# Reordering the projection and mix stages: variances in two halves among the casts, later projection, mixes two images ahead

## What is computed

```python
# projection stage: normalize over the 128 channels of each pixel, add, and project to 16 channels
xn = (x - mean(x)) / sqrt(var(x) + eps)      # per pixel, over channels
s = x + xn                                   # kept for the mix stage
pm = einsum('bchw,mc->bmhw', xn, w_in)       # 128 -> 16 channels
# (a stage between the two turns pm into xe: FFT, gain, inverse FFT)
# mix stage: back to 128 channels, add, normalize again
x1 = s + einsum('bmhw,cm->bchw', xe, w_out)  # 16 -> 128 channels
tn = (x1 - mean(x1)) / sqrt(var(x1) + eps)   # input of the next stage
total = tn.sum(pixels)                       # for the routing of the experts
```

## Time and profile before

| | us |
|---|---|
| median of 3 runs (lowest, highest) | 3659.25 (3657.81, 3667.75) |
| the profiled execution, its own time | 3660.29 |
| its span in the trace | 3658.5 |
| projection stage, about | 0 to 210 |
| mix stage, about | 412 to 641 |

### The profile page before, as it was taken

The page is one execution under the profiler, slowest core; times in us unless marked ns, Lnnn a source line. Parts: engine busy times, 40 slices in busy tenths (PEclk is TensorE's granted clock), DMA queues, the critical chain, the costliest instruction groups (busy, mean ns, idle before and its releaser), DMA issues. The chain is left out here.

```text
span 3658.5 us, 67013 instructions
## 1 busy us (share of the span) xinstructions
PE 3166.6 (87%) x27077; PEld 1711.9 (47%) x27136; DVE 1684.6 (46%) x2348; ACT 1527.2 (42%) x2263; POOL 810.3 (22%) x694
## 2 busy tenths in 40 slices
PE   5655676399999985999997879999999999999999
PEld 1155422255555542566665434546463545545444
DVE  5724256567677541111112254545454645545453
ACT  3411244167776661111223334545453444445433
POOL 2410232134444421111110112121212111121221
PEclk7767666699999985999998889999999999999999
DMA  5421364313334323777777311313132231313000
GB/s 187 154 75 23 121 257 196 157 46 138 147 147 164 153 115 123 187 212 214 214 207 236 123 56 52 127 46 128 51 104 81 76 109 41 110 43 125 12 12 23
DMA packets 192538, 438.59 MB, mean 120 GB/s; under 512 B 33341, under 2 KB 100157, under 8 KB 183741
## 3 DMA queue, kind: packets, MB, share of 16 engines
q1 hardware_dynamic: 192356, 436.20, 35.9%
HBM read 247.40 MB, written 188.75 MB: 119 GB/s over the span
## 5 line engine op out<-in xcount | busy, mean ns | idle before, releaser
L2113 DVE TENSOR_TENSOR d_hid_scaled<-d_hid_scaled,d_ps 128x512 f32<-128x512 f32 x512 | 331.3, 684 | 605.7 <-PE d_ps L1800 553.6
L1789 PE MATMUL d_ps<-d_hid_scaled,d_w 128*128 128x512 f32 x1024 | 526.4, 596 | 8.0 <-DVE d_X L2119 3.8
L1974 ACT ACTIVATE d_hid_scaled<-d_ps,d_b 128x512 f32<-128x512 f32 x512 | 349.9, 686 | 382.0 <-PE d_ps L1778 375.6
L1517 PE MATMUL c_ps<-c_pad,c_weight 32*32 32x512 f32 x13824 | 475.2, 601 | 26.2 <-ACT c_pad L1469 18.9
L1517 PEld LDWEIGHTS c_ps<-c_pad,c_weight 32*32 32x32 f32 x13824 | 287.1, 103 | 214.1 <-issue 129.7
L1776 PE MATMUL d_ps<-d_tnh,d_w1h 128*128 128x512 f32 x512 | 296.5, 579 | 9.2 <-ACT d_hid_scaled L1974 9.2
L1148 PE MATMUL b_ps<-b_hid,b_w2s 128*128 128x512 f32 x512 | 261.6, 595 | 0.0
L2061 POOL CAST d_tnh<-d_TN 128x512 fp32r<-128x512 f32 x64 | 39.9, 623 | 972.7 <-PE d_ps L1778 935.4
L1578 DVE COPY c_pad<-c_P 128x1024 f32<-128x1024 f32 x48 | 33.4, 696 | 414.9 <-PE c_ps L1517 379.2
L1789 PEld LDWEIGHTS d_ps<-d_hid_scaled,d_w 128*128 128x128 f32 x1024 | 195.5, 191 | 44.5 <-DVE d_hid_scaled L2113 2.3
L1469 ACT ACTIVATE c_pad<-c_P 128x1024 f32<-128x1024 f32 x48 | 51.8, 1080 | 392.7 <-PE c_ps L1517 372.0
(11 more groups left out here) (270 smaller groups left out, 5858.7 us busy)
## 6 DMA issues: line engine op xcount, KB each, us to landing
scratch_qkv<-b_qkv SPq DMA_DIRECT2D x64, 768.0 KB, 3.5
c_P<-scratch_qkv SPq DMA_DIRECT2D x192, 256.0 KB, 4.7
scratch_agg<-c_out SPq DMA_DIRECT2D x192, 256.0 KB, 5.0
d_buf<-scratch_qkv SPq DMA_DIRECT2D x96, 512.0 KB, 4.4
d_buf<-scratch_agg SPq DMA_DIRECT2D x96, 512.0 KB, 3.8
p_X<-in_x SPq DMA_DIRECT2D x8, 2048.0 KB, 7.5
scratch_s<-p_X SPq DMA_DIRECT2D x8, 2048.0 KB, 6.3
m_X<-scratch_s SPq DMA_DIRECT2D x8, 2048.0 KB, 7.7
```

The lines of the kernel that those rows point to most:

```text
L1517: end = nc.tensor.matmul(ps[on(i), k * QUADS + h, :].rearrange("p (b r w) -> p b r w", b=2, w=HB), weight[k][on(q), 2 * r + x, on(h)], pad ...
L1789: nc.tensor.matmul(moe_bank, w2[:, e, :], scaled[n % 3][:, :], start=False, stop=(e == E - 1)).then_inc(moe_pe, 1)
L1974: nc.scalar.activation(hid[n % 3][:, :], hid_bank(n), ACT.Gelu, bias=b1[:, n % E:n % E + 1]).then_inc(hid_done, 1)
L2113: nc.vector.tensor_tensor(scaled[n % 3][:, :], hid[n % 3][:, :], spread_bank(n), ALU.mult).then_inc(scaled_done, 1)
```

## The change

No instruction of the computation is added or removed. In the projection stage:

- `squares` gets 8 buffers instead of 4
- TensorE's body becomes: 8 casts of the mean of b, variances 0 to 3, inverse casts 0 to 3 of b-1, variances 4 to 7, inverse casts 4 to 7 of b-1, means of b+1, projection of image b-2 (before: b-1)
- ScalarE does deviations ahead of split 0 of b+1, and reads image b-2
- VectorE inverts after five scalings instead of six

In the mix stage:

- `X` and `XE` hold four images instead of three, and image b+4 is loaded when image b is stored and centred
- image b+2 is mixed in the body of image b, in pairs: after casts 0 to 3, after casts 4 to 7, after inverse casts 4 to 7, and at the end. Images 0 and 1 are mixed before the first body
- variances in two halves, with the inverse casts 0 to 3 of b-1, means of b+1, and inverse casts 4 to 7 between them
- ScalarE does split 1 of b-1 at the head of the body, and its reads in pairs among the squares
- VectorE scales all of image b-1 and does join 0 of b+1 before it inverts
- SyncE stores `X` of image b+2 and then `TN` of image b-1 in the turn of image b

The diff, cut to its core:

```diff
@@ projection: TensorE
                     for c in range(NCH):
                         norm.cast_mean(pe, b, c, mean_free(b))
+                    norm.variances(pe, b, range(4))
+                    for c in range(4):
+                        norm.cast_inverse(pe, b - 1, c, inverse_free(b - 1))
+                    norm.variances(pe, b, range(4, NCH))
+                    for c in range(4, NCH):
+                        norm.cast_inverse(pe, b - 1, c, inverse_free(b - 1))
                     if more:
                         means(b + 1)
-                    for c in range(4):
-                        norm.cast_inverse(pe, b - 1, c, inverse_free(b - 1))
-                    norm.variances(pe, b)
-                    for c in range(4, NCH):
-                        norm.cast_inverse(pe, b - 1, c, inverse_free(b - 1))
-                    project(b - 1)
+                    if b >= 2:
+                        project(b - 2)
@@ projection: ScalarE
+                    norm.deviations(act, b, eps)
                     if more:
                         norm.split(act, b + 1, 0)
-                    norm.deviations(act, b, eps)
                     norm.split(act, b, 1)
+                    if b >= 2:
+                        read(b - 2)
@@ projection: VectorE
-                    scale(b - 1, range(6))
+                    scale(b - 1, range(5))
                     norm.invert(dve, b)
-                    scale(b - 1, range(6, NCH))
+                    scale(b - 1, range(5, NCH))
@@ mix: SyncE
                 def next_load(b):
                     sp.wait_ge(x1_stored, b * 16 + 16)
                     norm.wait_centred(sp, b, NCH - 1)
-                    sp.wait_ge(loaded, b * 80 + 240)
-                    passed(sp)
-                    load(b + 3)
+                    sp.wait_ge(loaded, b * 80 + 320)
+                    load(b + 4)
...
+                sp.wait_ge(x1_stored, 16)
+                store_x1(1)
+                for b in range(B):
+                    if b + 4 < B:
+                        next_load(b)
+                    if b + 2 < B:
+                        sp.wait_ge(x1_stored, b * 16 + 32)
+                        store_x1(b + 2)
+                    if b:
+                        store_tn(b - 1)
@@ mix: TensorE
+                for b in range(B):
+                    for c in range(4):
                         norm.cast_mean(pe, b, c, mean_free(b))
+                    mixes(b + 2, (0, 1))
                     for c in range(4, NCH):
+                        norm.cast_mean(pe, b, c, mean_free(b))
+                    mixes(b + 2, (2, 3))
+                    norm.variances(pe, b, range(4))
+                    if b:
+                        for c in range(4):
+                            norm.cast_inverse(pe, b - 1, c, inverse_free(b - 1))
+                    if b + 1 < B:
                         means(b + 1)
+                    if b:
+                        for c in range(4, NCH):
+                            norm.cast_inverse(pe, b - 1, c, inverse_free(b - 1))
+                    mixes(b + 2, (4, 5))
+                    norm.variances(pe, b, range(4, NCH))
+                    mixes(b + 2, (6, 7))
@@ mix: ScalarE
+                for b in range(B):
+                    if b:
+                        norm.split(act, b - 1, 1)
+                    squares(b, (0, 1))
+                    reads(b + 2, (0, 1))
+                    squares(b, (2, 3, 4))
+                    reads(b + 2, (2, 3))
+                    squares(b, (5, 6, 7))
+                    if b + 1 < B:
+                        norm.split(act, b + 1, 0)
+                    reads(b + 2, (4, 5))
                     norm.deviations(act, b, eps)
+                    reads(b + 2, (6, 7))
@@ mix: VectorE
+                for b in range(B):
                     centre(b)
+                    if b:
+                        norm.join(dve, b - 1, 1)
+                        scale(b - 1, range(NCH))
+                    if b + 1 < B:
+                        norm.join(dve, b + 1, 0)
                     norm.invert(dve, b)
```

More of the change, by code:

```diff
@@ L740, in phase_mix @@
         y_pe, y_done, x1_done, total_done, total_stored = sem("y_pe"), sem("y_done"), sem("x1_done"), sem("total_done"), sem("total_stored")
-        third = lambda buf, b: buf[:, bass.ds((b % 3) * HW, HW)]
-        part = lambda buf, b: lambda c: buf[:, bass.ds((b % 3) * HW + c * CH, CH)]
+        image = lambda b: X[:, b % 4 * HW:(b % 4 + 1) * HW]
+        normed = lambda b: TN[:, b % 3 * HW:(b % 3 + 1) * HW]
+        x_part = lambda b: lambda c: chunk(image(b), c)
+        tn_part = lambda b: lambda c: chunk(normed(b), c)
+        rows = lambda b: slice(b % 4 * ROWS, (b % 4 + 1) * ROWS)
         ORDER = [chunk_of(g, w) for w in range(2) for g in range(4)]
@@ L760, in store_x1 @@
                     passed(sp)
[L761 removed]
+                    sp.dma_start(batch_of(d["x1"], b), image(b)).then_inc(x1_stored, 16)
                 def store_tn(b):
@@ L831, in means @@
                     pe.wait_ge(x1_done, b * NCH + NCH + 4)
-                    norm.means(pe, b, part(X, b))
-                def body(b, more):
-                    for c in range(NCH):
-                        norm.cast_mean(pe, b, c, mean_free(b))
-                        if more:
-                            mix(b + 1, c)
-                    for c in range(4):
-                        norm.cast_inverse(pe, b - 1, c, inverse_free(b - 1))
-                    norm.variances(pe, b)
-                    for c in range(4, NCH):
-                        norm.cast_inverse(pe, b - 1, c, inverse_free(b - 1))
-                    if more:
-                        means(b + 1)
@@ L847, in _ @@
-                for i in range(NCH):
-                    mix(0, i)
-                means(0)
-                for c in range(NCH):
-                    norm.cast_mean(pe, 0, c, mean_free(0))
-                    mix(1, c)
-                norm.variances(pe, 0)
-                means(1)
-                for b in range(1, B - 1):
-                    body(b, True)
-                body(B - 1, False)
+                    norm.means(pe, b, x_part(b))
+                for b in range(2):
+                    for i in range(NCH):
+                        mix(b, i)
+                    if b == 0:
+                        means(0)
@@ L871, in read, with squares, reads @@
                     nc.scalar.activation(Y[i % 4][:, :], banks[6 + i % 2][:, :], ACT.Copy).then_inc(y_done, 1)
-                def body(b, more):
-                    for c in range(NCH):
-                        norm.squares(act, b, c, part(TN, b), lambda c: norm.wait_centred(act, b, c))
-                        if more:
-                            read(b + 1, c)
-                    norm.deviations(act, b, eps)
-                    norm.split(act, b, 1)
-                    if more:
-                        norm.split(act, b + 1, 0)
-                for i in range(NCH):
-                    read(0, i)
-                norm.split(act, 0, 0)
-                for b in range(0, B - 1):
-                    body(b, True)
-                body(B - 1, False)
+                for b in range(2):
+                    for i in range(NCH):
+                        read(b, i)
+                    if b == 0:
+                        norm.split(act, 0, 0)
+                def squares(b, cs):
+                    for c in cs:
+                        norm.squares(act, b, c, tn_part(b), lambda c: norm.wait_centred(act, b, c))
+                def reads(b, some):
+                    for i in some:
+                        if b < B:
+                            read(b, i)
+                for b in range(B):
[9 more added lines that the diff above has]
+                    reads(b + 2, (4, 5))
+                    norm.deviations(act, b, eps)
+                    reads(b + 2, (6, 7))
+                norm.split(act, B - 1, 1)
             @block.gpsimd
```

53 lines of the change are left out of this document (17 added, 36 removed).

## The result

The changed kernel takes **3575.6 us** (median of 4 runs, 3573.71 to 3577.24), the kernel before 3663.5 in the same comparison: a ratio of 0.9759, with an interval of 0.9737 to 0.9780. A second comparison, of five rounds, gave 3582.45 against 3661.56, a ratio of 0.9786 (0.9773 to 0.9798). The profiled execution took 3575.71 us, its span is 3573.9 against 3658.5. Medians and ratios here are of fast runs alone; one of the six runs of reads_first, 4110.79 us at a granted clock of 0.72, is left out as slow.

The account below looks back on a forecast made before the run. No engine is full; both stages are bound by a chain passing from engine to engine once per image. Projection -31.7 and mix -40 against 3660.29 us give 3588.6, stated as 3588, range 3566 to 3608.

Parts of the forecast that it names:

- no change: Mix stage: pairs of mixes stay together but each stands alone on TensorE; mix +24 us, in all 3653; chance 0.03.
- slower: Mix stage: mixes no longer overlap in pairs, each waiting for its own read; mix +94 us, in all 3723; chance 0.02.
- (a) to (c): Projection stage: eight square buffers, TensorE's new order, and later means and projection give a natural period of 16.4 us.
- (d): Projection stage: each load waits for an older image's projection and small stores, closing a loop of 19.4 us per image.
- small stores 0.97 behind T: Projection stage, sign of the load loop: small stores issue 0.97 us after VectorE starts centring an image (T).
- the load loop does not bind: Projection stage: small stores issue quickly; projection -38 to -44 us, in all 3582 to 3576; both faster rivals together 0.25.
- (e): Mix stage start: all eight mixes of image 1 run before image 0 is centred, so first centring comes 8.8 us later.
- (f): Mix stage body, step by step with all of TensorE at the lower clock level: a period of 19.8 us.
- (g): Mix stage clock: means, last pair and last variances at the higher level give about 17.2 us; 18.0 taken.
- mix at the higher level: Mix stage: TensorE halves its share, body about 16 us; -50 to -52, in all near 3577; both faster rivals together 0.25.
- (h): Mix stage transfers: 20.8 us per image one after the other, over the new period, yet costing 0 with some 10 us of cover.
- (i): Mix stage end: images 6 and 7 have no mixes, so about 16.0 us between their centrings; the tail stays.

Follow-up runs that it names:

- reads_first: Changed kernel, but in the mix stage ScalarE reads the first pair of mixes before the older image's second split, with five squares together: 3584.0 us.
- root_behind: Changed kernel, but in the projection stage ScalarE does the split of the next image's means ahead of the square root again: 3605.3 us.
- store_late: Changed kernel, but SyncE waits for the projection's read-out before the 2 MB store, so small stores follow the large one again: 3597.1 us.
- mix_singly: Changed kernel, but in the mix stage each cast of the mean alternates with one mix, and each square with one read: 3615.3 us.

## Why the prediction was right, and where a term was off

**The sign, the size and the cause held.** 3575.6 lies in the range of 3566 to 3608, 12.4 below the forecast. Both stages were bound by a chain and not by an engine; the chains got shorter by the steps named, and neither "no change" nor "slower" came near.

**(a) to (c), the natural period of 16.4: right in sum, with two errors that cancel.** Measured 16.4 for images 2 to 4. Scaling starts at T+6.0 (5.8 forecast), the root at 7.9 (7.7), the reciprocal at 9.0 (8.9), the joins at 14.0 (14.0). But the two joins take 2.4 us and not the 1.4 that I took from the mix stage, and the cast of the next mean runs beside the second of them instead of adding its 0.93. The kernel before had shown the price in this very stage, 3.07 us for two in the earlier trace rows themselves, and 3.06 on VectorE's timeline of image 2, with GpSimd adding beside them.

The sum also rests on the clock. It had TensorE at the lower level until T+15.5, although means and projection began half a microsecond later than it said; 16.4 held because one or both ran at the higher level. In the body of T_5, with means of 3.50 and a projection of 1.89, the next cast waited only 0.59 us for its join, so a projection of 3.4 as in the earlier trace rows would have cost about 1 us more there (an estimate from these rows). root_behind shows that the root's place ahead of the split is a condition of this period, which the sum had used without saying what it was worth.

**(d), the load loop: the step that failed.** The loop exists, but a turn of it takes 16.8 to 17.7 us and not 19.4. From load 6 to load 7 (100.81 to 117.64) it is 7.98 to the means, 7.01 from there to the first small store, 1.73 for the four, and 0.11. The forecast had 7.5, 7.97 (7.0 + 0.97), 3.74 and 0.2. The small stores are 2.0 of the difference: I took 3.74, kept 2.1 as the bound, and they took 1.73, below the bound. The text had the mechanism, a large store just ahead of them, and store_late shows that it is the right one. Means and projection are 1.0, the projection now at the higher clock. The landing went the other way: from issue to the means it was 9.05 for load 5 and 8.78 for load 7, where I took the median of the earlier trace rows, 7.5.

So the loop is about level with the natural period, touches it from image 5 on, and costs 1.6 us in all (periods 16.6, 16.6 and 17.6). The sign that I had named, small stores 0.97 behind T, did not come either: they were issued 0.3 to 1.6 us ahead of T, so that load 4 left 0.2 us behind T_3 and not 4.0, and T_4 was not held. That is 3.0 of the 10.4 us between forecast and measured; the three periods from T_4 to T_7, 50.8 against 58.2, are 7.4. The rival "the load loop does not bind" is nearly what happened: -44 by its natural end, -42.05 measured, -31.7 forecast. The tail was right, 27.3 us from T_7 to the last store (26.6).

**(e), the start: +7.1 against +8.8.** Eight mixes do stand ahead of T_0. But two of the four pairs ran at the higher clock, which the sum of 2.93 each had not allowed for:

```profile
398.12 1.41 PE L815 MATMUL m_ps<-m_XE,m_w_out 16*128 16x512 f32 x4
400.41 1.58 PE L815 MATMUL m_ps<-m_XE,m_w_out 16*128 16x512 f32 x4 [0.88 <-ACT m_Y L882]
```

**(f) and (g), the body: 18.2 on average over the first six against 18.0, by a partly different chain.** The clock did what (g) said: 0.66 over the stage against 0.60, 0.74 in the body shown, with means of 2.24 between the 1.92 and 3.64 of the earlier trace rows. That fits the rule of the Trainium skill cited there in its direction only: fed more densely, TensorE was granted the higher clock more often, but not throughout, and the rival "mix at the higher level" did not come about. The projection stage does not fit it even in direction: from T_0 to T_7 TensorE's busy share rose from 65% to 76%, and its granted clock went from 0.73 to 0.71. The body of 20.0 us is one whose means ran at the lower level, at 3.56, so that the fifth scaling waited 1.75 for the inverse cast behind them.

What I did not have is the join at 1.35 for 0.75. It put VectorE's own list level with the root. That this is what made the body insensitive to one engine alone is my reading, not a result of its own.

**(h), transfers: they cost 0, as argued.** The DMA engines are 97% busy in the body shown. Two waits of the bodies are put down to a load, 2.40 and 2.63 us of GpSimd's additions at 428.31 and 482.49, and they are no longer than the same idle time at 446.82 and 464.66 (2.63), where a read of ScalarE ends it. **(i):** the last period was 15.8 (16.0), and the tail behind T_7 grew by 1.2, for which I had nothing. In all M is -38.9 against -40.

**The sum.** -42.05 and -38.94 stand against -31.7 and -40; the remaining 3.6 of the span's 84.6 belong to stages that move as much with nothing changed.

## What to carry to other kernels

Before pricing a group of small DMA issues, look for a large store just ahead of them in the same queue: the same instructions cost less than half as much seven microseconds behind it, and a reordering can move them from one case to the other. In a stage bound by a chain, a shorter chain packs TensorE more densely, which brought a higher mean clock in one stage here and not in the other, so price the groups behind the edit at both levels and keep both in the range. And compare stages between fixed marks of the trace: here the medians alone would have hidden effects of 3 to 5 us under a remainder that moves by 9.

## What the hardware did that I had not expected

The issue of a small store on SyncE took 1.21 us in the median right behind a 2 MB store (store_late, 3.86 for four) and 0.42 seven microseconds behind one (1.73 for four). Small loads behind a 2 MB load alone cost 2.0 to 2.4 for four.

A join on VectorE, whose two tensor inputs lie in SBUF, takes 0.75 us alone, and 1.34 in the median of the changed kernel's mix bodies, where GpSimd adds beside it. Centring (0.67) and scaling (0.68), which take one input from PSUM, are not slowed. The page "SBUF — State Buffer" of the Trainium skill, section "SBUF: two separate sides", says that VectorE and GpSimd share one pair of ports, that a VectorE operation with two SBUF inputs needs it against a GpSimd operation that reads SBUF, and that the loser waits the whole time out. The runs agree as to which operations suffer, and on how long. In the body shown, GpSimd's row beside the first join (466.37, 1.35 us, done at 467.72) is this:

```profile
464.66 2.51 POOL L921 TENSOR_TENSOR m_X<-m_X,m_Y 128x512 f32<-128x512 f32 x2 [2.63 <-ACT m_Y L882]
```

The second addition of this row ends at 467.17, and the join 0.55 later. It is so for 22 of the 23 joins of the changed kernel that start during an addition: whatever was left of the addition, the join ends 0.55 us behind it (the 23rd, of 1.82 us, sat through the next addition too). That is why such a join takes anything from 0.79 to 1.75. The other way round, in mix_singly, five joins of the mix stage started first: they kept 0.75, and the addition that started beside each took 1.73 instead of 1.25.

In the mix stage of the kernel before, all sixteen joins kept their 0.75, and around the two ahead of T_3 (at 512.61 and 513.67) GpSimd stood idle for 13.1 us: a reordering that puts two engines beside each other should be priced for this.
